# Means and roots of the experts' rows: measured by the experts, or carried to them from the routers

## The reference

```python
def layernorm(x):  (x - mean(x)) / sqrt(var(x) + 1e-5)

def moe(x):                                  # used before and after the middle
    logits = x @ w_switch + b_switch         # 8 experts
    routes, pmax = argmax, max of softmax(logits)
    pos = how many earlier rows (this one included) chose the same expert, less 1
    keep = pos < 256                         # capacity of an expert
    y = relu(rows_of_expert @ w1[e] + b1[e]) @ w2[e] + b2[e]     # 256 -> 1024 -> 256
    out = y of the row's slot if keep else x
    return out * pmax / pmax

x = x + 0.5 * moe(layernorm(x))
x = x + middle(layernorm(x))                 # linear attention, then an MLP 256 -> 1024 -> 256
x = x + 0.5 * moe(layernorm(x))
```

## Time and profile before

| | |
|---|---|
| three timed runs, median (lowest to highest) | 694.62 us (694.18 to 695.31) |
| the profiled execution, its own time | 692.72 us |
| its span, from the first to the last instruction | 691.0 us |
| mean granted TensorE clock | 0.976 of full speed |
| busy: PE, DVE, ACT, POOL | 648.0, 517.4, 462.8, 367.4 us |

### The profile page before, as it was taken

One profiled execution on the slowest core, in us unless ns is written; L12 is line 12 of the kernel. 1 busy time (PEld: TensorE's weight loads), 2 busy tenths in 40 slices (PEclk: granted clock), 3 DMA queues, 4 the chain that ended last, 5 costly groups with the idle time before them and its releaser, 6 DMA issues.

```text
span 691.0 us, 18005 instructions
## 1 busy us (share of the span) xinstructions
PE 648.0 (94%) x6398; PEld 570.5 (83%) x6398; DVE 517.4 (75%) x1371; ACT 462.8 (67%) x923; POOL 367.4 (53%) x542
## 2 busy tenths in 40 slices
PE   7789999997789999999999999999999994999997
PEld 5559998975679898988888888888988783899997
DVE  7968797624678877868778778888767558799982
ACT  6687777605467786767767667776763654798882
POOL 5254454634867545464673764845635653454422
PEclk9789999999999999999999999999999996999999
DMA  8499979424765555544565565564451534577750
GB/s 262 140 295 309 289 220 333 142 80 81 112 112 98 97 95 78 116 73 76 103 90 122 80 97 122 69 115 83 64 115 26 174 101 108 176 221 240 225 166 31
DMA packets 284803, 95.61 MB, mean 138 GB/s; under 512 B 213988, under 2 KB 281664, under 8 KB 284714
## 3 DMA queue, kind: packets, MB, share of 16 engines
q1 hardware_dynamic: 267610, 82.27, 49.4%
q0 software_dynamic: 4992, 11.47, 6.0%
q10 hardware_dynamic: 12112, 0.72, 1.1%
HBM read 65.09 MB, written 29.40 MB: 137 GB/s over the span
## 4 chain that ended last, share of the span: by engine, by line
PE 51%; DVE 8%; POOL 5%; issue 5%; ACT 3%; SPq 3%; DMA 1%; ACTq 1%; POOLq 0%; DVEq 0%
PE bank L1990 46%; PE bank L1999 5%; SPq L453 2%; POOL hids L920 2%; DMA qkv_rows<-feats 1%; SPq L459 1%; DVE den L1810 1%; DVE kv_ L1835 1%; DVE hn_ L1855 1%; DVE att_ L1808 1%; POOL sth L905 1%; ACTq L453 1%; POOL stz L889 1%; DVE ots L1801 0%; DVE feats L1930 0%
## 5 line engine op out<-in xcount | busy, mean ns | idle before, releaser
L1990 PE MATMUL bank<-hnts,up_w 128*128 128x512 f32 (+1 forms) x432 | 106.1, 382 | 0.1
L1990 PE MATMUL bank<-down_w,hids 128*128 128x256 f32 x768 | 104.5, 284 | 1.2 <-POOL hids L920 0.4
L920 POOL TENSOR_TENSOR hids<-hid,hids 128x512 fp32r<-128x512 f32 (+1 forms) x67 | 82.0, 1225 | 36.3 <-ACT hids L1212 36.2
L1990 PEld LDWEIGHTS bank<-down_w,hids 128*128 128x128 f32 x768 | 96.6, 189 | 4.2 <-POOL hids L920 1.8
L1990 PEld LDWEIGHTS bank<-hnts,up_w 128*128 128x128 f32 x432 | 71.3, 189 | 10.3 <-ACT hids L1212 0.3
L1990 PE MATMUL bank<-qkv_w,xnts 128*128 128x256 f32 (+1 forms) x384 | 76.9, 348 | 2.9 <-DVE xnts L1821 2.4
L1990 PEld LDWEIGHTS bank<-qkv_w,xnts 128*128 128x128 f32 x384 | 60.6, 189 | 20.0 <-issue 5.8
L1207 ACT ACTIVATE hid<-bank,cols 128x512 f32<-128x512 f32 (+1 forms) x72 | 45.7, 640 | 39.8 <-PE bank L1990 39.4
L886 POOL TENSOR_SCALAR stz<-stz 128x1 f32<-128x1 f32 x32 | 7.2, 226 | 115.2 <-DVE stz L1839 115.2
L1990 PE MATMUL bank<-xa_xt,a_w 128*128 128x256 f32 x384 | 52.6, 287 | 1.6 <-ACT xa_h L1048 1.1
L1990 PE MATMUL bank<-xb_xt,b_w 128*128 128x256 f32 x384 | 50.2, 280 | 0.7 <-DVE xb_xt L1502 0.5
(11 more groups left out here) (299 smaller groups left out, 1637.7 us busy)
## 6 DMA issues: line engine op xcount, KB each, us to landing
qkv_rows<-feats SPq DMA_DIRECT2D x32, 384.0 KB, 2.7
a_raw<-in_L_ffn_w_dram SPq DMA_DIRECT2D x32, 256.0 KB, 4.6
a_w<-in_L_ffn_w_dram SPq DMA_DIRECT2D x32, 256.0 KB, 4.7
b_raw<-in_L_ffn_w_dram SPq DMA_DIRECT2D x32, 256.0 KB, 3.4
b_w<-in_L_ffn_w_dram SPq DMA_DIRECT2D x32, 256.0 KB, 3.2
mid_rows<-x_all SPq DMA_DIRECT2D x8, 512.0 KB, 4.5
values<-qkv_rows SPq DMA_DIRECT2D x32, 128.0 KB, 3.0
late_rows<-x_ SPq DMA_DIRECT2D x8, 512.0 KB, 3.1
```

The costliest lines, as they stand in the source:

```text
L920: pool.tensor_tensor(hids[1][u % 3][:, 0:w], hid[u % 2][:, 0:w], f32(hids[0][u % 3][:, 0:w]), ALU.subtract).then_inc(s_hidl, 1)
L1990: return pe.matmul(dst, left, right, start=start, stop=stop, skip_group_check=True)
```

## The change

The experts no longer measure. Mean and root, made once by the router, travel to the slots with row number and factor.

- **A.** The roots are kept in `mv_a`. POOL splits mean and root of all 32 tiles into three bf16 parts (`part_norms`, four instructions over 64 values) and multiplies them with the one-hot for each batch (`left_norms`, one instruction over 16 x 8 x 6 = 768 values, twice). PE multiplies the marks with that (`norm_slots_a`, 64 matmuls of 48 columns); DVE sums the parts (`norms_a`).
- **B.** A table entry holds four numbers instead of two. For the last two groups POOL makes the parts (`part_norms_b`, 192 values in the product), PE the sums (`slot_norms`, 16 matmuls), and DVE adds them to the table (`norms_b`). Statistics are written into the entries.
- **The experts.** `measure_rows`, `root_rows` and `root_half` are gone; `norm_half` normalises as soon as a half's rows are there. POOL loads both halves of the second expert's rows at once.
- **Moved.** `factor_parts_late` of both late groups goes behind the first expert's rows, `slot_factors` of both to PE behind the second `up`, and `slots_b` behind that. ACT passes tiles 28 to 31 of B behind its two `turn_half`. In A, ACT's eight tiles in `turn_half` are gone: ACT does groups 4 and 5, DVE groups 6 and 7, within the first four pairs. `idle_products` are 3 instead of 5 (A) and 9 instead of 0 (B) ahead of the first half, and 1 and 2 instead of 4 and 2 behind the halves.

```diff
@@ POOL
+            def part_norms(given, parts, rest, step):
+                high, middle, low = (parts.rearrange("p t (v f) -> p t v f", f=3)[:, :, :, i] for i in range(3))
+                pool.tensor_copy(high, given).then_inc(s_parts, 1)
+                pool.wait_ge(s_parts, step + 1)
+                pool.tensor_tensor(rest, given, high, ALU.subtract).then_inc(s_parts, 1)
+                pool.wait_ge(s_parts, step + 2)
+                pool.tensor_copy(middle, rest).then_inc(s_parts, 1)
+                pool.wait_ge(s_parts, step + 3)
+                pool.tensor_tensor(low, rest, middle, ALU.subtract).then_inc(s_parts, 1)
+
+            def part_norms_b(g):
+                these, step = slice((g - NG + 2) * GROUP, (g - NG + 3) * GROUP), parted_norms(5 * (g - NG + 2))
+                pool.wait_ge(s_broot, 2 * (g + 1))
+                pool.wait_ge(s_parts, step)
+                part_norms(entry_of(g)[:, :, 2:4], norm_parts_b[:, these], norm_rest_b[:], step)
+                pool.wait_ge(s_parts, step + 4)
+                pool.wait_ge(s_bpick, 7 * (g + 1))
+                wide = [P, GROUP, E, 6]
+                pool.tensor_tensor(left_norm_b[:, these], hot_b[g % 2][:].unsqueeze(3).broadcast_to(wide),
+                                   norm_parts_b[:, these].unsqueeze(2).broadcast_to(wide), ALU.mult).then_inc(s_parts, 1)
...
                 load_rows(ex.first, ex)
-                load_rows(ex.first + 1, ex, range(0, 1))
-                for s in range(ST):
-                    root_half(s, ex)
-                    if s == 0 and ex.first == 0:
-                        pass_factors(1)
-                load_rows(ex.first + 1, ex, range(1, ST))
-                root_rows(ex.first + 1, ex)
+                load_rows(ex.first + 1, ex)
+                if ex.first == 0:
+                    pass_factors(1)
...
+            def left_norms(b):
+                these, wide = slice(b * BATCH, (b + 1) * BATCH), [P, BATCH, E, 6]
+                pool.wait_ge(s_parts, 4)
+                pool.wait_ge(s_apick, 8 * b + 7)
+                pool.tensor_tensor(left_norm_a[:, these], hot_a[:, these].unsqueeze(3).broadcast_to(wide),
+                                   norm_parts[:, these].unsqueeze(2).broadcast_to(wide), ALU.mult).then_inc(s_parts, 1)
             for g in range(NG):
                 roots_a(g)
+            pool.wait_ge(s_art, 2 * NG)
+            part_norms(mv_a[:], norm_parts[:], norm_rest[:], 0)
+            pool.wait_ge(s_amark, BATCH)
+            left_norms(0)
+            left_norms(1)
             pass_factors(0)
@@ DVE
+            def norm_half(x, s, ex):
+                c = (x - ex.first) * ST + s
+                dve.wait_ge(ex.sem.rows[x % ROWS_AHEAD][s], 16 * (x // ROWS_AHEAD + 1))
+                dve.tensor_scalar(ex.buf.unit[x % 2][:, s], ex.buf.rows[x % ROWS_AHEAD][:, s], ex.buf.norms[:, c, 0:1],
+                                  ex.buf.norms[:, c, 1:2], ALU.subtract, ALU.mult).then_inc(ex.sem.unit, 1)
...
-                measure(0)
-                if meanwhile:
-                    meanwhile(0, 1)
-                norm(0)
-                measure(1)
+                dve.wait_ge(ex.sem.norms, 3 if x else 1)
+                norm_half(x, 0, ex)
+                meanwhile(0, 1)
+                norm_half(x, 1, ex)
                 low(0)
...
             def behind_rows(first, end):
-                if first == 0:
+                if first == 1:
+                    factor_parts_late(NG - 2)
                     factor_parts_late(NG - 1)
-                if first == 1:
+            def behind_pairs(u):
+                if u == E * PAIRS + 1:
                     slots_b()
...
             tokens_b()
+            norms_b()
...
             def middle_weights(u):
+                if u < 2 * ST:
+                    if u == 0:
+                        dve.wait_ge(s_apass, 8)
+                    for n in range((NG - 2) * GROUP + 2 * u, (NG - 2) * GROUP + 2 * u + 2):
+                        dve.tensor_scalar(x_all[:, n], x_all[:, n], small_a[:, 8, n:n + 1], small_a[:, 7, n:n + 1],
+                                          ALU.mult, ALU.add).then_inc(s_apass, 1)
@@ PE
-                    idle_products(4 - 2 * s)
+                    idle_products(1 + s)
...
+                    if ex.first == E and u == E * PAIRS + 1:
+                        slot_factors(NG - 2)
+                        slot_factors(NG - 1)
...
             number_slots_a(1)
+            norm_slots_a(0)
+            norm_slots_a(1)
...
-            run_experts(xa, 5)
+            run_experts(xa, 3)
...
-            slot_factors(g - 1)
-            idle_products(3)
-            slot_factors(g)
+            slot_norms(g - 1)
+            slot_norms(g)
             pe.wait_ge(s_bpos, 4)
-            run_experts(xb, 0)
+            run_experts(xb, 9)
```

More of the change, by code:

```diff
@@ L19 @@
 CAP_FACTOR = 0.5
-ExpertBufs = namedtuple("ExpertBufs", "table slot token scale rows unit stat mean_var rstd xts h fin hs")
-ExpertSems = namedtuple("ExpertSems", "table token rows stat root unit turned xt xtl up relu down fin sent "
+ExpertBufs = namedtuple("ExpertBufs", "table slot token scale norms rows unit xts h fin hs")
+ExpertSems = namedtuple("ExpertSems", "table token rows norms unit turned xt xtl up relu down fin sent "
                                       "got1 got2 high1 low1 hlow biased")
@@ L163, in build @@
         s_bpos, s_bmark, s_blate, s_bslot = sem("b_places_and_slots"), sem("b_marked"), sem("b_late_factors"), sem("b_slotted")
-        one = {f: sem(f"experts_{f}") for f in ("table", "token", "stat", "root", "unit", "turned", "xt", "xtl",
+        one = {f: sem(f"experts_{f}") for f in ("table", "token", "norms", "unit", "turned", "xt", "xtl",
                                                 "up", "relu", "down", "fin", "high1", "low1", "hlow", "biased")}
@@ L998, in logits_out_b, with pass_in_place @@
                 act.copy(lgt_b[:], src[:, 0:P]).then_inc(s_blge, 1)
+            def pass_in_place(g):
+                act.wait_ge(s_bfac, 4 * (g + 1))
+                act.wait_ge(s_x2s[g % 2], 16 * (g // 2 + 1))
+                for i in range(GROUP):
+                    row = x2[:, g % 2 * GROUP + i]
+                    act.activation(row, row, ACT.Identity, bias=fac_b[g % 2][:, 2, i:i + 1],
+                                   scale=fac_b[g % 2][:, 3, i:i + 1]).then_inc(s_bplace, 1)
             def soften(g):
@@ L2044, in slot_numbers, with slot_norms @@
                 last.then_inc(s_bslot, 1)
+            def slot_norms(g):
+                sums = norm_sums_b.rearrange("p (e s f) -> p s e f", s=ST, f=6)
+                pe.wait_ge(s_parts, parted_norms(5 * (g - NG + 3)))
+                for n in range(g * GROUP, (g + 1) * GROUP):
+                    i = n - LATE_FROM
+                    for s in range(ST):
+                        last = mm(sums[:, s], mark_b[i][:, s * P:(s + 1) * P], left_norm_b[:, i], i == 0 and s == 0,
+                                  n == NT - 1)
+                last.then_inc(s_bslot, 1)
             def slot_factors(g):
@@ L2055, in slot_factors, with norm_slots_a @@
                 last.then_inc(s_bslot, 1)
+            def norm_slots_a(b):
+                sums = norm_sums_a.rearrange("p (e s f) -> p s e f", s=ST, f=6)
+                pe.wait_ge(s_parts, 5 + b)
+                for n in range(b * BATCH, (b + 1) * BATCH):
+                    for s in range(ST):
+                        last = mm(sums[:, s], mark_a[n][:, s * P:(s + 1) * P], left_norm_a[:, n], n == 0 and s == 0,
+                                  n == NT - 1)
+                    last.then_inc(s_aslot, 1)
             def factor_slots_a(b):
```

183 lines of the change are left out of this document (76 added, 107 removed).

## The result

The changed kernel takes 704.3 us in its median (four runs, 701.76 to 706.39) against 694.96; the ratio is 1.0127, 95% interval 1.0102 to 1.0152. Timed again later, beside the kernel before each time, it gave 1.0083 (1.0061 to 1.0105) and 1.0107 (1.0075 to 1.0139). It is slower by 6 to 9 us. The prediction said 694.0, with "slower" at 0.18.

A forecast was written before the change was run, and what follows sets the result against it. PE, full within the experts, was taken as the bound, so only the starts of A's and B's experts count. A +1.1 (-1.8 behind the tokens, +2.9 ahead) and B -1.65, taken as -0.6, gave 694.0 us; range 691.0 to 696.6.

The forecast's parts named there:

- "slower": Whole kernel: the case that the change turns slower by over 0.2%, or 1.4 us; chance 0.18.
- its rows are all asked for at once: A, second expert: its rows need only DVE's `norm_rows` and come before PE wants them, so PE's wait goes: -1.15 us.
- B's start: B, tokens to first `up`: the second gather's landing, not DVE, ends last; `up` at 588.9 instead of 591.07, -2.1 us.
- My third rival: A, ahead of the tokens: POOL's products are longer than predicted; at 3.7 us each the whole is +3.5, 698.1; chance 0.18.
- ACT's and DVE's parts of the pass-through are off the path: A, behind the tokens: ACT loses eight tiles, DVE gains eight of 0.4 us in the first four pairs; no cost counted.
- A, ahead of the tokens: POOL's two 768-value products, 1.84 us each, hold DVE up, and `part_norms` adds 0.2: tokens later by 2.9 us.
- A, from the tokens to `up`: 64 mean products take 2.8 us, first half's turn unchanged; from turn to `up` 3.0 us instead of 3.64: -0.6.
- one of the signs of being wrong that I had named: Start of `up`: the prediction counts as wrong if PE starts `up` at the low clock.
- B: Tokens +0.8 for POOL's parts and product, yet first `up` -2.1; `slot_factors` in a full PE +0.45: -1.65 us in all.
- the -0.6 forecast: Whole kernel: A +1.1 and B -1.65, taken as -0.6 us, to 694.0 us; chance 0.47, own range 692.8 to 695.3.

The follow-up runs named there:

- e1: Changed kernel, but POOL's gathers for each stage's third and fourth expert wait until DVE has normalised the second expert's rows: 696.7 us, ratio 1.0034 to the kernel before.
- e10: The changed kernel itself, timed and profiled again beside the kernel before: 701.5 us, ratio 1.0083.
- e18: Changed kernel with only two waits on POOL, holding the second expert's gathers and the third and fourth's: 694.7 us, ratio 0.9987 to the kernel before.
- e3: Changed kernel, but tiles that no expert takes are passed through as in the kernel before: 699.8 us, ratio 1.0058 to the kernel before.
- e9: The kernel before itself, run and profiled again: 695.3 us, ratio 0.9986.
- e5: Kernel before, but third and fourth expert's gathers issued right behind the second expert's last, five in a row: 696.6 us, ratio 1.0034.
- e13: The kernel of e5 again, in another group of runs: 699.3 us, ratio 1.0041 to the kernel before.
- e6: Changed kernel with third and fourth experts' gathers held, one signal a batch, passes as before, both POOL products behind the second batch's hot rows: 691.7 us, ratio 0.9957.
- e16: The kernel of e6 again, in another group of runs: 692.0 us, ratio 0.9922 to the kernel before.
- e7: Changed kernel with third and fourth experts' gathers held, one signal a batch, passes as before, second expert's gathers behind its means and roots: 691.6 us, ratio 0.9947.
- e15: The kernel of e7 again, in another group of runs: 693.1 us, ratio 0.9953 to the kernel before.
- e8: e6 and e7 together, with five idle products ahead of A's first half and two behind each half: 692.5 us, ratio 0.9955 to the kernel before.
- e17: e6 and e7 together, the changed kernel with all cures: 692.1 us, ratio 0.9947 to the kernel before.

## Why the prediction was wrong

**The step that failed** is the one on the gathers. I wrote of the second expert that "its rows are all asked for at once", took 1.15 us for it, and likewise priced B's start by the second gather's landing. That eight gathers now stand in a row on POOL, with no root between them, had no price in the sum and was no rival. In the changed kernel's trace PE's signals come late in these rows. The one for A's second half is 2.7 us late (49.32 against 46.58): with what follows from it, A's first `up` comes 13.65 us behind the tokens, where it is 10.24 in e1, and its 36 products take 5.81 us for e1's 4.51, at the low clock. The one for B's first relu is 3.4 us late (606.29 against 602.91): from B's tokens to the end it is 110.9 us, where it is 108.2 in e1. The one for the mean sums makes DVE stand 2.94 us, but costs PE no more than its wait of 0.54. Together these differences are 7.4 us, and 5.9 by e10's trace in place of this one. e1 holds half of the gathers and takes most of it away: 1.0083 to 1.0127 becomes 1.0034. e18 has no loss left, but in circumstances in which the changed kernel was not measured. My third rival had the right sign for another reason.

**The second failed step** is "ACT's and DVE's parts of the pass-through are off the path". They are, on ACT and DVE; I didn't follow SP's queue, where stores wait for those tiles and weights wait behind the stores. By e3's window it is 2.2 to 3.3 us.

**A, ahead of the tokens**, came out near in sum, in part by luck: 2.9 predicted, 2.7 measured (2.4 by e10 against e9). The products cost 1.54 us (13.11 less 11.57, the same in every trace with this order) where I had 2.7: they take 1.47 and 1.64, not 1.84, and the second meets only a wait of 0.4, as DVE had gone on to instructions that it doesn't stop. The rest stands ahead of the first marks and is not shown to be the change's. From `choose_a(0)`'s first instruction to these marks it is 4.45 us against 3.74, but it is 4.46 in e9, e5 and e13 as well, which have no `part_norms`: there DVE waits for PE's counts. `part_norms` itself stretched three of DVE's instructions by 0.28 us in all (0.29 became 0.33, 0.42 and 0.40), near my 0.2, where its four instructions last 1.2 us.

**A, from the tokens to `up`**: the 64 mean products took 2.72 us for my 2.8, and PE's queue stood as worked out. Where the second stall is gone (e1) `up` is at 46.95, where I had 46.6: from the first half's turn to `up` it is 3.4 us, not 3.0, as the clock rose only at about 47, later than I had taken. In the changed kernel it was low until 53, and PE started `up` at the low clock, one of the signs of being wrong that I had named. The wait for the second expert's rows was gone, as predicted.

**B**: tokens to `up` 7.47 us for my 7.2, and the tokens lost nothing to POOL's products (2.66 us behind the hot rows, 2.68 before) where I had 0.8. With the stall gone B gains 2.0 us from the tokens on in e1. In e18 it is 1.1, as the clock was low again behind the start of `up` (0.50 from 596 to 599 us). I had 2.45 from the tokens on, and 1.65 in all.

So the terms that I priced came out near, and what was missing was the terms that I did not look for. The -0.5 us of e18 (interval -2.8 to +1.0) against the -0.6 forecast is no confirmation: the measured parts, with the queue's 2.2 to 3.3 us, add up to somewhere between 0 and +4 us; e1 lies there, at +2.4 by its ratio.

**What stays open.** Which part of the chip delays PE's signals, and why the stalls without releaser are seen only where the trace holds few landing events; whether the recording of the trace itself plays a part was not tested. The changed kernel never ran in a group with 16 events a landing, so whether it is slow there too is not known. The kernels with held gathers gave like ratios in both (e6 and e16, e7 and e15), and so did the kernel before with five gathers in a row (e5 and e13), with and without a late signal. Not every signal during a gather is late (e13 in B, e9), so the length of the row is not the whole condition.

## What to carry to other kernels

When an edit takes small instructions out from between DMA issues on one engine, ask what the issues do when they stand in a row, and give each only as much lead as its consumer needs: here one wait on POOL (e1) was worth 0.5% to 0.9%. Before a stall is given a price, look whether the engine behind it had other work: DVE's 2.94 us cost PE 0.54. Follow a moved instruction to every queue that waits for it, the DMA queues above all, since a store that waits holds the loads behind it. And if the same edit is to be judged by its trace, profile the reference beside it on the same chip: e5 alone would have made me drop a theory that e1 and e13 bear out, and e18 alone would have made it look proven. Without e9 I would have put 0.7 us on four instructions that did not cost them.

## What the runs showed of the hardware

While POOL issued indirect DMAs back to back (0.95 us each, 0.30 between), or up to 1.1 us behind such a row, semaphore signals of PE reached DVE and ACT 1.6 to 3.6 us behind the end of the product that they tell of, as the profile has that end (0.01 us for the first `up` of B in the kernel before), and PE itself stood for up to 1.62 us with nothing shown that it waits for. Signals of DVE and ACT were not late: in the kernel after DVE's half ends at 44.06 and PE turns it at 44.11, ACT's copy ends at 45.20 and DVE goes on at 45.24. The late signals were seen in 12 of the 13 traces with few landing events (all but e9), and in none of the seven with 16, though six of those (e5 to e8, e17, e18) have four or five gathers in a row at A's start.

A POOL product of 768 bf16 values with both operands repeated takes 1.47 us where DVE's instruction stands for it from its start, and 1.61 to 1.65 where it starts beside a DVE instruction at work. It stops DVE instructions with two operands in SBUF (0.29 becomes 1.47) and also a mark, which reads one bf16 operand (0.28 becomes 0.93). The Trainium skill, "SBUF — State Buffer", section "Who interferes with whom", lists `tensor_scalar` among the operations that can enter a two-port mode and contend; the mark agrees.
